# Feed-forward experts turned so that their rows lie on the partitions, with group weights multiplied in by GpSimd

## The chip, the cores and the metric

One NeuronCore of one Trainium2 chip runs the whole program. The metric is device microseconds of one execution, median of the runs; a profiled execution gives the trace. The engines are TensorE (PE, with its weight loads shown as PEld), VectorE (DVE), ScalarE (ACT), GpSimd (POOL) and SyncE (SP), which here issues all DMAs. All matrix products are done in float32r by splitting each operand into a high and a low part and adding three products (high x high, high x low, low x high).

## The reference

Input x is 4 batches of 1024 tokens of 256. First a multi-head latent attention block with 16 heads is added to x; it is not touched by the change but for its last body. Then comes the feed-forward part on the layer norm of the result, for each token n:

```
scores = softmax(x @ gate_w.T)                     # 64 experts
w_e    = the 8 largest of scores, 0 elsewhere
flat   = w_e[:, inv_map]                           # 8 groups of 8
scalar = flat.sum(-1)                              # one weight per group
soft   = softmax(where(flat == 0, -1e9, flat), -1)
xg     = x[:, None, :] + einsum('ngi,ghi->ngh', soft, mask_up_w)
g, u   = xg @ gate_proj, xg @ up_proj              # 176 rows per group
d      = (silu(g) * u) @ down_proj
y      = sum over g of scalar[g] * d[g]
```

The 8 groups of 176 rows make 1408 = 11 x 128 rows. The kernel computes the gate and up product of xg as x times the weights plus soft times a small product of mask_up_w and the weights (the "mask weights", `mw`), made once at the start.

## The kernel before

`attention_prepare` and `attention` do the attention (lines 66 to 1562), `ffn` (line 1565 on) the rest. `attention` is written as bodies 0 to 32, one per pair of heads, in which each engine works through a list written out by hand (TENSOR, VECTOR, SCALAR, POOL, SYNC); the last body has lists of its own (TENSOR_LAST and so on, line 1004), which also hold the router steps R(0) to R(6) of the first half-batch, the splitting of the first quad of expert weights into high and low (QUAD), the mask product of that quad (MASK) and the statistics of the second half-batch (STATS). SP loads the second quad's weights at line 1258 and then stores the last batch's sums.

`ffn` works on 32 tiles of 128 tokens; four tiles are a half-batch H (8 of them), for which the router runs as a unit. Tokens lie on the partitions. For a tile i, PE does for each group g six matmuls of 352 columns (gate and up rows of the group side by side, `gate_up`, line 1652), the tile of x being the stationary operand. After four groups `soft` (line 1662) adds the mask part with four matmuls that use 32 rows each and run side by side. ScalarE takes the silu (line 1758), and VectorE multiplies gate, up and the token's group weight in one instruction (`gates`, line 1815; the group weight is one number per partition). For the down product the result has to be turned: `transposes` (line 1673) has PE turn 11 blocks of 128x128 into one bank, in steps of 4, 4 and 3; ScalarE copies the high part out (`high`, line 1764), VectorE subtracts to get the low part (`low`, line 1823), and PE does 11 x 3 matmuls of 256 columns (`down`, line 1689). VectorE adds the tile to x (`add_up`) and SP stores a half-batch at a time.

The order on PE is that of the loop at line 1706: gate/up of groups 0 to 7 of tile i, with the transposes and the down product of tile i-1 between them. The router's steps for the next half-batches are put between them by tables (PE_AT, ACT_AT, DVE_AT, line 1612) that give each step a tile and a place. The router's steps are `router_tensor`, `router_scalar` and `router_vector` (lines 672 to 808): PE parts 0 and 1 turn the normalised x, 2 makes the logits, 3 turns the selected weights, 4 gathers them by group, 5 and 6 turn the soft weights; VectorE's part 4 (lines 773 to 779) ends the softmax and finds the top 8, part 5 (lines 781 to 785) selects, part 6 makes the group weights, part 7 the soft weights. Layer norm is GpSimd's: `router_root` and four `router_norm` (lines 828 to 841); it does nothing else in this part apart from two subtractions at the start (line 1874).

## Time and profile before

| | us |
|---|---|
| median of 3 runs (1659.49 to 1663.20) | 1661.84 |
| the profiled execution's own time | 1660.86 |
| its span, first to last instruction | 1658.8 |
| PE busy in the span | 1565.8 |
| VectorE busy | 1181.2 |
| ScalarE busy | 814.4 |
| GpSimd busy | 806.3 |
| feed-forward part, from PE's first matmul at 1160.87 to the end | 497.9 |

Busy times are sums over one engine; they overlap with each other. A matmul's end is modelled, so durations of consecutive matmuls overlap: the distance between two starts is what a matmul costs. GpSimd's and ScalarE's times are as recorded.

### The profile page before, as it was taken

The numbers are of one execution on the slowest core, as the hardware profiler recorded it, in microseconds if no ns is written. First come the engines' busy times: TensorE is split into PE (matmuls) and PEld (weight loads), VectorE is DVE, ScalarE is ACT, GpSimd is POOL, SyncE is SP. The second block draws the span as 40 slices with busy tenths as digits, with TensorE's granted clock in tenths as the row PEclk, the third lists the DMA queues.
The fourth block names the chain that finished last, engine by engine and source line by source line (L and its number), as shares of the span: only waits on it lengthen the run. The fifth ranks groups of instructions, "written<-read, shape, count | busy, mean of one in ns | idle before, by whom it ended". The sixth has DMA issues, their size and how long they took to land. (4 is left out here: it accounts for less than half of the span.)

```text
span 1658.8 us, 69237 instructions
## 1 busy us (share of the span) xinstructions
PE 1565.8 (94%) x30224; PEld 1343.1 (81%) x30224; DVE 1181.2 (71%) x2780; ACT 814.4 (49%) x1902; POOL 806.3 (49%) x673
## 2 busy tenths in 40 slices
PE   5689999999999999999999999997999999999998
PEld 4568878877778777877877878875899999999998
DVE  6778878887788778878877888886645446445443
ACT  6555555555556555555555555543433333333332
POOL 4376767676667666676767676762010010011000
PEclk9889999999999999999999999998999999999999
DMA  9523221112231112222112311112100000000000
GB/s 299 130 71 79 55 54 45 52 41 73 72 77 53 48 51 77 64 64 73 55 45 63 93 42 42 45 39 77 59 27 1 26 27 1 26 27 1 13 14 13
DMA packets 83981, 91.87 MB, mean 55 GB/s; under 512 B 33696, under 2 KB 58272, under 8 KB 83680
## 3 DMA queue, kind: packets, MB, share of 16 engines
q1 hardware_dynamic: 83680, 87.44, 18.5%
q8 instruction: 240, 3.93, 1.0%
q14 instruction: 61, 0.50, 0.1%
HBM read 55.67 MB, written 14.94 MB: 43 GB/s over the span
## 5 line engine op out<-in xcount | busy, mean ns | idle before, releaser
L1395 ACT ACTIVATE probs<-aps,nmax 128x896 f32<-128x896 f32 (+7 forms) x512 | 378.1, 740 | 410.3 <-DVE nmax L1443 398.4
L1443 DVE CUSTOM_DVE_ANT_0 aps<-aps,mask_row 128x896 f32<-128x896 f32 (+7 forms) x512 | 380.7, 759 | 122.9 <-PE aps L46 119.4
L46 PE MATMUL aps<-kTh,qh 128*128 128x512 f32 (+3 forms) x768 | 291.2, 379 | 13.7 <-DVE ql L1131 7.2
L1122 POOL TENSOR_TENSOR rot<-rot,sinT 64x512 f32<-64x512 f32 x126 | 160.4, 1273 | 292.7 <-DMA rot<-rot 292.7
L46 PE MATMUL aps<-pT_second,vrep 32*64 32x128 f32 (+1 forms) x15616 | 263.5, 260 | 26.2 <-issue 23.3
L46 PEld LDWEIGHTS aps<-pT_second,vrep 32*64 32x64 f32 x15616 | 224.8, 131 | 66.1 <-issue 53.7
L1453 DVE STREAM_TRANSPOSE pT_second<-probs 128x896 f32<-128x896 f32 (+3 forms) x256 | 264.0, 1032 | 4.7 <-ACT probs L1395 4.5
L46 PE MATMUL aps<-kTl,qh 128*128 128x512 f32 (+3 forms) x768 | 259.2, 345 | 1.6 <-issue 1.6
L46 PE MATMUL aps<-kTh,ql 128*128 128x512 f32 (+3 forms) x768 | 223.2, 345 | 0.0
L46 PEld LDWEIGHTS aps<-kTh,qh 128*128 128x128 f32 x768 | 145.5, 189 | 75.0 <-issue 38.9
L1826 DVE TENSOR_TENSOR aTl<-fps,aTh 128x512 fp32r<-128x512 f32 (+1 forms) x96 | 61.9, 646 | 167.3 <-ACT aTh L1769 167.3
L46 PE MATMUL fps<-wth,qh 128*128 128x352 f32 x512 | 176.1, 344 | 3.7 <-PEq L848 3.7
L1769 ACT CAST aTh<-fps 128x512 fp32r<-128x512 f32 (+1 forms) x96 | 52.8, 551 | 235.7 <-PE fps L1685 235.6
L1453 DVE STREAM_TRANSPOSE pT_first<-probs 128x256 f32<-128x256 f32 (+3 forms) x256 | 124.1, 495 | 59.1 <-ACT probs L1395 58.9
L46 PE MATMUL fps<-wtl,qh 128*128 128x352 f32 x512 | 166.1, 324 | 0.0
L46 PE MATMUL fps<-wth,ql 128*128 128x352 f32 x512 | 165.8, 324 | 0.0
L831 POOL TENSOR_SCALAR f_vareps<-f_aggr 128x4 f32<-128x4 f32 x8 | 1.9, 233 | 336.1 <-DVE f_aggr L759 336.1
L1125 POOL TENSOR_TENSOR rot<-rot 64x512 f32<-64x512 f32 x126 | 160.4, 1273 | 9.9
L1131 POOL TENSOR_TENSOR ql<-rot,qh 128x512 fp32r<-128x512 f32 x126 | 159.7, 1285 | 7.4 <-ACT qh L1384 7.4
L1123 POOL TENSOR_TENSOR rot<-rot,cosT 64x512 f32<-64x512 f32 x126 | 161.3, 1280 | 0.0
L46 PEld LDWEIGHTS aps<-kTl,qh 128*128 128x128 f32 x768 | 146.6, 191 | 12.4 <-issue 0.2
L46 PEld LDWEIGHTS aps<-kTh,ql 128*128 128x128 f32 x768 | 137.2, 191 | 8.9
(195 smaller groups left out, 3032.9 us busy)
## 6 DMA issues: line engine op xcount, KB each, us to landing
rot<-rot SPq DMA_DIRECT2D x256, 64.0 KB, 2.5
linv_b<-inverses_scratch SPq DMA_DIRECT2D x128, 128.0 KB
wqs<-wq_scratch SPq DMA_DIRECT2D x30, 256.0 KB, 3.6
raw_numbers<-in_x SPq DMA_DIRECT2D x8, 512.0 KB, 6.4
vrep<-values_scratch SPq DMA_DIRECT2D x16, 256.0 KB, 4.6
inverses_scratch<-linv_t SPq DMA_DIRECT2D x256, 1.0 KB
acc<-in_x SPq DMA_DIRECT2D x16, 256.0 KB, 3.2
x_scratch<-acc SPq DMA_DIRECT2D x16, 256.0 KB, 3.1
```

Source lines behind the costliest of these rows:

```text
L46: return nc.tensor.matmul(out, lhsT, rhs, start=start, stop=stop, skip_group_check=True)
L831: pool.tensor_scalar(t.vareps[:], t.aggr[:, :, 1], EPS, None, ALU.add).then_inc(t.ve, 1)
L1122: eng.tensor_tensor(rot2[:, k, :], rot2[:, k, :], t.sinT[:, cols], ALU.mult).then_inc(q_turned, 1)
L1123: eng.tensor_tensor(rot1[0:64, k, :], rot1[0:64, k, :], t.cosT[0:64, cols], ALU.mult).then_inc(q_turned, 1)
L1125: eng.tensor_tensor(rot1[0:64, k, :], rot1[0:64, k, :], rot2[:, k, :], ALU.add).then_inc(q_add, 1)
L1131: eng.tensor_tensor(ql[:, a, cols], rot1[:, rot_slot(x, r), :], qh[:, a, cols].bitcast(F32), ALU.subtract).then_inc(q_split, 1)
L1395: nc.scalar.activation(probs[:, SLOT[x, r], 0:w], sps[:, at:at + w], ACT.Exp, bias=nmax[:, c, a, j:j + 1], scale=-1.0, accum_out=lsum[:, c ...
L1443: nc.vector.tensor_tensor_reduce(out=s, in0=s, in1=mask[:, N - PW[c][j]:N], scale=-1.0, scalar=3.0e38, op0=ALU.add, op1=ALU.min, accum_out ...
L1453: nc.vector.transpose(pT[c][:, a, 0:w // S32, j * S32:(j + 1) * S32], probs[:, SLOT[EXP(c, a, j), r], 0:w].rearrange("p (b k) -> p b k", k ...
L1769: nc.scalar.copy(aTh[:, i % 2, m.start:m.stop, :].rearrange("p m n -> p (m n)"), turned_in(i, q)[:, 0:len(m) * P]).then_inc(aT_h, 1)
L1826: nc.vector.tensor_tensor(aTl[:, i % 2, m.start:m.stop, :].rearrange("p m n -> p (m n)"), turned_in(i, q)[:, 0:len(m) * P], aTh[:, i % 2, ...
```

## The change

In the feed-forward part tokens move to the free axis. The work is cut into 8 half-batches x 11 blocks of 128 expert rows = 88 blocks (n = 11 H + m). For a block PE multiplies the block's 128 gate rows (stationary) with 512 tokens, six matmuls of 512 columns, then the same for its up rows; `soft` adds the mask part with one full-height matmul of 512 columns for each (two for block 5, which has rows of groups in both halves of the soft weights). For that the mask weights are laid out with zeros in all rows but those of a block's groups (`mwz`, in the space of the attention's keys). 8 of the blocks lie in a single group; blocks 4, 5 and 10 are put together from three, four and three groups (MIXED). The down product needs no transposes: its stationary operand is the block's product, 128 tokens at a time, 4 x 3 matmuls of 256 columns, added up over 11 blocks in two banks. It follows two blocks behind (LAG).

The group weight is now different along the free axis, so it can't be one number per partition. VectorE multiplies up and silu (`gate`), GpSimd multiplies the result with a spread tile of weights (`weigh`), ScalarE rounds it to the high part, VectorE subtracts for the low part. The spread tiles come by DMA: VectorE's part 6 turns the group sums in squares of 32, SP writes them to DRAM in 4 DMAs and reads them back spread over the partitions, 18 DMAs per half-batch. The router's steps get a block in place of a tile (`router_parts`); the statistics of the half-batch after next come at block 8, its layer norm on GpSimd at blocks 9 and 10. The mask products are taken over column ranges (pure groups 256 columns, mixed blocks 2 x 48). The first quad's weights are loaded in three pieces, not four, and the down weights are loaded in attention's last body.

The diff, cut to its core:

```diff
+WORDS = [5 * KC * GB, 6 * KC * GB]
+FIRST_QUAD, SECOND_QUAD = (0, 2, 1), (1, 0, 2, 3)
+MIXED = {4: [(0, slice(0, 48), P), (1, slice(48, 96), P), (2, slice(96, P), P)],
+         5: [(2, slice(0, 16), 160), (3, slice(16, 64), P), (4, slice(64, 112), P), (5, slice(112, P), P)],
+         10: [(5, slice(0, 32), 144), (6, slice(32, 80), P), (7, slice(80, P), P)]}
+SOFT = [[(0, m)] for m in range(5)] + [[(0, 5), (1, 5)]] + [[(1, m)] for m in range(5)]
...
 def mask_products(nc, t, q, bank):
-        for gg in range(4):
-            last = mm(nc, bank[32 * gg:32 * gg + 32, 0:GU], t.mu4[:, k, g, :], columns(part, g, k).bitcast(F32),
+        for g, m, first, width, at in mask_windows(q):
+            last = mm(nc, to, t.mu4[:, k, g, :], both_columns(part, m, k, slice(first, first + width)).bitcast(F32),
...
+def mask_clear(nc, t, q):
+    nc.gpsimd.memset(t.kTh[:, q, :].bitcast(F32), 0.0).then_inc(t.mw_zero, 1)
+    nc.gpsimd.memset(t.kTl[:, q, 0:2 * GB].bitcast(F32), 0.0).then_inc(t.mw_zero, 1)
+def mask_spread(nc, t, q):
+            nc.gpsimd.tensor_copy(to, src).then_inc(t.mw_rdy, 1)
+            copied += 1
+            nc.gpsimd.wait_ge(t.mw_rdy, copied)
+def keep_mass(nc, t, H):
+    nc.sync.wait_ge(t.mass_turned, H + 1)
+    to = t.mass_dram[H % 2].rearrange("g (t a i) -> a (g t) i", a=4, i=32)
+    for a in range(4):
+        nc.sync.dma_start(to[a], t.massT[32 * a:32 * a + 32, :]).then_inc(t.mass_kept, 16)
...
+        if H > 0:
+            dve.wait_ge(t.mass_kept, 64 * H)
+        dve.transpose(t.massT[:], t.mass[:, H % 2]).then_inc(t.mass_turned, 1)
...
             load_experts(nc, t, ins, 1, slice(0, 4))
+            sp.wait_ge(t.first_low, len(PIECES[0]))
+            sp.dma_start(t.raw_d, ins["down"].rearrange("(m p) d -> p m d", p=P)).then_inc(t.down_loaded, 16)
+            keep_mass(nc, t, 0)
             all_added(LAST - 1)
...
+        PE_AT = {0: 0, 1: 1, 2: 2, 3: 4, 4: 5, 5: 8, 6: 9}
+        ACT_AT = {0: 0, 1: 1, 2: 3, 3: 4, 4: 6, 5: 8, 6: 9}
+        DVE_AT = {1: 0, 2: 1, 3: 2, 4: 3, 5: 3, 6: 5, 7: 6}
...
+            def spread_mass(H, m):
+                if H > 0:
+                    sp.wait_ge(weighted, (H - 1) * MC + m + 1)
+                for g, rows, _ in MEMBERS[m]:
+                    row = t.mass_dram[H % 2, g]
+                    sp.dma_start(mass_b[rows, m, :], row.partition_broadcast(rows.stop - rows.start))\
+                        .then_inc(mass_loaded[m], 16)
...
+            def products(n, u):
+                if n >= 2:
+                    pe.wait_ge((silu_done, act_done)[u], n - 1)
                 for k in range(KC):
+                    for j, (x, w) in enumerate(((t.xTh, t.wth), (t.xTh, t.wtl), (t.xTl, t.wth))):
+                        mm(nc, banks[:, 2 * (n % 2) + u, :], columns(w, m, k, u), x[:, k, tok(H)], k == 0 and j == 0, False)
+            def soft(n, u):
+                for q, e in entries:
+                    last = mm(nc, banks[:, 2 * (n % 2) + u, :], t.mwz[q][e][:, u * P:(u + 1) * P], t.sT[:, q, tok(H)],
+                              False, (q, e) == entries[-1])
+            def down(n):
+                pe.wait_ge(aT_l, n + 1)
+                for i in range(HT):
                     for j, (a, w) in enumerate(((aTh, dh), (aTh, dl), (aTl, dh))):
+                        last = mm(nc, y_of(i), a[:, n % SLOTS, i * P:(i + 1) * P], w[:, m, :], m == 0 and j == 0 and i % 2 == 0,
+                                  m == MC - 1 and j == 2)
...
+                elif n < TOTAL:
+                    for u in range(2):
+                        products(n, u)
+                        soft(n, u)
+                    parts(n)
+                if n >= LAG:
+                    down(n - LAG)
...
+            for n in range(TOTAL):
+                silu(n)
+                if n > 0:
+                    high(n - 1)
+                parts(n)
...
+            def gate(n):
+                dve.wait_ge(up_ps, n + 1)
+                dve.wait_ge(silu_done, n + 1)
+                if n >= SLOTS:
+                    dve.wait_ge(aT_h, n - SLOTS + 1)
+                nc.vector.tensor_tensor(act_sb[:, n % SLOTS, :], banks[:, 2 * (n % 2) + 1, :], sg[:, n % SLOTS, :],
+                                        ALU.mult).then_inc(act_done, 1)
+            def low(n):
+                dve.wait_ge(aT_h, n + 1)
+                nc.vector.tensor_tensor(aTl[:, n % SLOTS, :], act_sb[:, n % SLOTS, :],
+                                        aTh[:, n % SLOTS, :].bitcast(F32), ALU.subtract).then_inc(aT_l, 1)
...
+            def weigh(n):
+                pool.wait_ge(act_done, n + 1)
+                pool.wait_ge(mass_loaded[m], 16 * len(MEMBERS[m]) * (H + 1))
+                nc.gpsimd.tensor_tensor(act_sb[:, n % SLOTS, :], act_sb[:, n % SLOTS, :], mass_b[:, m, :], ALU.mult)\
+                    .then_inc(weighted, 1)
...
+            for n in range(TOTAL):
+                weigh(n)
+                if m in (9, 10) and H + 2 < HALVES:
+                    if m == 9:
+                        router_root(nc, t, H + 2)
+                        pool.wait_ge(t.xT_ps, 2 * H + 4)
+                    for i in range(2 * (m - 9), 2 * (m - 9) + 2):
+                        router_norm(nc, t, H + 2, i)
```

VectorE's loop runs gate(n), low(n-1), then the router parts of block n, and at block 1 the four sums of the half-batch before.

## Rows read from the trace of the kernel before

**Rows 1.** The page's part 1, busy time by engine.
```profile
PE 1565.8 (94%) x30224; PEld 1343.1 (81%) x30224; DVE 1181.2 (71%) x2780; ACT 814.4 (49%) x1902; POOL 806.3 (49%) x673
```
**Rows 2.** Windows: stretch, length, busy by engine, granted clock, DMA share, GB/s.
```profile
1242.43:1303.96 61.53, 60.92 (x444) 57.29 (x443) 31.51 (x93) 22.38 (x55) 6.81 (x6) 1.00 0.06 18
...
1640.00:1659.00 19.00, 14.01 (x106) 12.81 (x104) 6.07 (x15) 3.83 (x12) 0.00 (x0) 1.00 0.05 15
```
**Rows 3.** PE groups by form, 1242.43 to 1303.96: busy, mean ns, idle before.
```profile
L46 PE MATMUL fps<-dh,aTh 128*128 128x256 f32 x44 | 13.2, 300 | 0.6 <-DVE aTl L1826 0.6
```
**Rows 4.** Timeline of PE, 1249 to 1255: start, length, what.
```profile
1249.78 0.28 PE L46 MATMUL fps<-dh,aTh 128*128 128x256 f32 x1
...
1250.84 0.32 PE L46 MATMUL fps<-wth,qh 128*128 128x352 f32 x1
...
1253.74 0.60 PE L1685 MATMUL fps<-ident,act_sb 128*128 128x128 f32 x4
1254.27 0.44 PE L46 MATMUL fps<-mw,xq 32*128 32x352 f32 x4
1254.63 0.43 PE L46 MATMUL fps<-wth,qh 128*128 128x352 f32 x1
1254.90 0.32 PE L46 MATMUL fps<-wtl,qh 128*128 128x352 f32 x1
```
**Rows 5.** The chain that ended last, 1227 to 1228: start, length, what.
```profile
1227.23 0.44 PE fps L1685 x4
```
**Rows 6.** Timeline of PE in attention, 603 to 604.
```profile
602.97 1.09 PE L46 MATMUL aps<-xq,wqs 128*128 128x512 f32 x4
603.89 0.40 PE L46 MATMUL aps<-kTh,qh 128*128 128x512 f32 x1
```
**Rows 7.** Groups by form: VectorE and ScalarE 1183 to 1645, GpSimd whole span.
```profile
L1826 DVE TENSOR_TENSOR aTl<-fps,aTh 128x512 fp32r<-128x512 f32 x61 | 42.1, 691 | 112.7 <-ACT aTh L1769 112.7
...
L1769 ACT CAST aTh<-fps 128x512 fp32r<-128x512 f32 x61 | 35.8, 587 | 172.9 <-PE fps L1685 172.9
...
L1541 POOL TENSOR_TENSOR ol<-o,oh 128x512 fp32r<-128x512 f32 x64 | 82.5, 1288 | 32.4 <-ACT oh L1405 32.4
```
**Rows 8.** Timelines of VectorE and GpSimd at 1163, and VectorE at 1284.
```profile
1162.84 2.94 DVE L807 TENSOR_TENSOR rot<-mask_row,soft_h 128x256 f32<-128x256 f32 x2
...
1163.00 2.50 POOL L1874 TENSOR_TENSOR wtl<-raw_numbers,wth 128x1024 fp32r<-128x1024 f32 x1 [11.53 <-DVE rot L804]
...
1284.27 0.76 DVE L807 TENSOR_TENSOR rot<-mask_row,soft_h 128x256 f32<-128x256 f32 x2
```
**Rows 9.** Timeline of VectorE: first and last of router parts 4 and 5.
```profile
1190.02 0.42 DVE L774 TENSOR_REDUCE r<-mask_row 128x4 f32<-128x256 f32 x1
...
1191.81 0.06 DVE L63 MEMSET f_spot_v<- 1x1 f32 x1
...
1196.33 0.08 DVE L782 MATCH_VALUE_LOAD mask_row<-top,mask_row 128x8 f32 x1
...
1197.23 0.42 DVE L785 TENSOR_TENSOR mask_row<-mask_row 128x256 f32<-128x256 f32 x1
```
**Rows 10.** Timeline of GpSimd at one layer norm: root's first step, the four norms.
```profile
1133.95 0.23 POOL L831 TENSOR_SCALAR f_vareps<-f_aggr 128x4 f32<-128x4 f32 x1 [5.71 <-DVE f_aggr L759]
...
1135.41 4.96 POOL L840 TENSOR_SCALAR cosT<-x,f_aggr,f_rstd 128x256 f32<-128x256 f32 x4
```
**Rows 11.** Timeline of PE: mask products of groups 4 to 7, and what follows.
```profile
1168.58 0.80 PE L46 MATMUL fps<-wth,mu 128*32 128x352 f32 x8
...
1171.09 0.43 PE L46 MATMUL fps<-wth,qh 128*128 128x352 f32 x1
```
**Rows 12.** Timeline at the end: PE's last matmul, VectorE's last add.
```profile
1655.84 0.28 PE L46 MATMUL fps<-dh,aTl 128*128 128x256 f32 x1
1656.16 0.42 DVE L1834 TENSOR_TENSOR x<-fps,x 128x256 f32<-128x256 f32 x1 [2.37 <-PE fps L46]
```

468 lines of the change are left out of this document (223 added, 245 removed).

## The prediction

> **What bounds the kernel now.** I read the page first, then the stretch of the feed-forward part (1161 us to the end) by windows, by groups and by time. On the page TensorE (PE) is busy for 1565.8 us of a span of 1658.8 us [rows 1]. In the feed-forward part one half-batch (512 tokens, four tiles) takes the 61.53 us from 1242.43 to 1303.96, of which PE is busy 60.92 us at a granted clock of 1.00 (2.4 GHz); VectorE has 31.5 us, ScalarE 22.4 us and GpSimd 6.8 us of work in it [rows 2]. Only 0.6 us of idle stands in front of the down matmuls [rows 3]. So this part costs what PE issues, and the change is to be priced by PE's pace, then by whether the other engines still keep ahead of it. Ends of matmuls are modelled, so I take distances between starts: nine 256-column down matmuls fill 1249.78 to 1250.84, 0.118 us each, and eighteen 352-column ones 1250.84 to 1253.74, 0.161 us each [rows 4]. Four transposes take 0.44 us [rows 5].
>
> **PE, per half-batch.** Before: 4 tiles x 8 groups x 6 = 192 gate/up matmuls of 352 columns, 192 x 0.161 = 30.9 us. After: 11 blocks x 2 x 6 = 132 of 512 columns. 512-column matmuls run in attention: four from 602.97 to 603.89, so 0.230 each [rows 6]; I take 0.232, and 132 x 0.232 = 30.6 us. The columns are the same (67,584) and so, almost, is the time: minus 0.3 us.
> The 44 transposes of the products go away, since the products now come out with the expert rows on the partitions: minus 11 x 0.44 = 4.8 us.
> The eight soft-mask groups were four 32-row matmuls each, which ran side by side: 0.36 us from 1254.27 to 1254.63. The matmul behind each took 0.27 us instead of 0.16, and the four transposes ahead of it 0.53 us instead of 0.44 [rows 4, 5]. So 8 x (0.36 + 0.11 + 0.09) = 4.5 us go. In their place come 24 full-height matmuls of 512 columns (twelve windows, gate and up): plus 24 x 0.232 = 5.6 us. Here the change pays: zero rows are multiplied too.
> The down product stays at 132 matmuls of 256 columns, the router's steps keep their instructions. The 0.6 us wait before down matmuls should go, as there are now two blocks between a product and its use.
> Sum: -0.3 - 4.8 - 4.5 + 5.6 - 0.6 = **-4.6 us per half-batch**, 8 x 4.6 = 36.8 us.
>
> **The new chain per block.** PE needs 14 x 0.232 + 12 x 0.118 = 4.66 us for a block. Call T(n) the time at which block n's up product is complete. Its products are needed by the down matmuls that PE reaches at T(n+2), 9.3 us later. Nearest rows: VectorE's 128x512 with one operand in PSUM 0.69, ScalarE's cast 0.59, GpSimd's 128x512 multiply-like operation 1.29 [rows 7]. VectorE's product is done at T(n) + 0.7, GpSimd's at + 2.0, ScalarE's high part after its silu of block n+1 at about + 4.2, VectorE's low part after the gate of n+1 at + 6.0. That leaves 3 us, so a plain block does not stall.
>
> **Where VectorE and GpSimd meet.** The new low part (act_sb minus aTh) reads two operands in SBUF, and begins just when GpSimd's multiply of the next block, with two SBUF operands as well, is released. The row to read is VectorE's pair of 128x256 subtractions at 1162.84, both operands in SBUF: 2.94 us for two that elsewhere take 0.76 us together; it ends at 1165.78, just behind GpSimd's 2.50 us operation, 1163.00 to 1165.50 [rows 8]. So I let the two exclude each other, first come first served: GpSimd's multiply ends at T(n) + 2.65, still inside the slack. The Trainium skill, "SBUF — State Buffer", section "Who interferes with whom", states it so: a VectorE instruction with two SBUF inputs and a GpSimd one that reads SBUF take turns, the second blocked for the whole of the first. The trace agrees (2.94 us against 0.76); by the rule as by the row the sum holds the two stalls that follow, and with ports of their own it would be that of the first rival. Two places remain where this reaches PE:
> (a) Block 3, router top-k. VectorE does gate, low part, part 4 and part 5, and PE's part 3 waits for the result at T(4) = T(3) + 4.66. Part 4 takes 1.85 us and part 5 1.3 us [rows 9]; gate and low part take 1.4 us, and the first two-operand step of part 4 (due at T(3) + 2.05) waits for GpSimd until about T(3) + 2.65, a loss of 0.6 us. Result at T(3) + 5.2 or a little later: PE waits 0.6 us, 7 times = **+4.2 us** (0 to 1.5 each).
> (b) Blocks 9 and 10, layer norm of the half-batch after next on GpSimd. Root takes 1.5 us and four norms 5.0 [rows 10], now mixed with two multiplies: multiply of 9 ends at T(9) + 2.65, root at + 4.15, two norms at + 6.65, multiply of 10 (behind VectorE's low part, which has waited for the second norm) at + 8.65, two norms at + 11.15. PE's transposes of it stand at T(9) + 2 x 4.66 + 0.44 = + 9.8. PE waits 1.35 us, for six half-batches = **+8.1 us** (0 to 2.5 each).
>
> **Data movement.** The group weights now go by DMA: VectorE turns the 128x32 masses in 32x32 squares, 4 issues put them to DRAM, then 18 spreading reads per half-batch (2.9 MB) fetch them, issued on SP from block 5 on and due from the next half-batch's block 0. That is five blocks, 23 us, to spare. On SP they stand behind the store and load of x, whose next user is block 8's statistics, and each read waits for the multiply that last used its tile, in the order of the blocks. I cost them nothing. If one is late, GpSimd's multiply stands first, and behind it ScalarE, VectorE and PE. In the last attention body SP waits for the turned masses ahead of the last stores of x; VectorE makes them before the adds that these stores wait for, so nothing again. The down weights are loaded in that body, behind the expert loads, and not in the feed-forward part: they were hidden and stay so.
>
> **Start and end.** The mask products for groups 4 to 7 cover 256 + 96 + 96 = 448 columns in place of 352, in the same side-by-side form; they took 2.5 us, 1168.58 to 1171.09 [rows 11], so +0.7 us. The first blocks share their engines with the expert splitting, 18 small mask copies on GpSimd, each waited for, and a clear. The trace has no such copy. Below, they cost nothing; above, 18 at the 1.29 us of rows 7 for the widest are 23 us, of which a block's slack hides at least 15, so 8 us. I take +0.3 us, near the low end because the narrow ones have a quarter of the partitions, PE has 18 to 24 matmuls to do first, and the first tile's present waits go. Together +1.0 us. At the end, PE's last matmul starts at 1655.84, one add of 0.42 us follows at 1656.16, and the span ends at 1658.8 [rows 12]. Now four adds stand there (+1.3 us). PE is idle for some 2.1 us in the last tile (5.0 us of the last 19, less the 2.9 after its end [rows 2]) and will be for 1.2 us, before the last block's down product: -0.9. Together +0.4 us.
>
> **Sum.** 1658.8 - 36.8 + 4.2 + 8.1 + 1.0 + 0.4 = 1635.7 us of span. The profiled execution took 1660.86 us, 2.1 us more than its span, and lies 1 us below the median of the runs (1661.84). So 1637.8 to 1638.8; I say **1638 us**. About 0.2% (3.3 us) is what a measurement of this kernel can tell from no change.
>
> **Rivals.**
> 1. No stall of (a) and (b): GpSimd and VectorE fall into another order, or PE's own small losses cover them. 1638 - 12.3 = about 1625 us. For: the times above are within 1 us of cover. Against: (b) counts busy time of GpSimd, not only waits. 0.22.
> 2. The 512-column matmuls are slower here than in attention, or block-wise switches between product, soft and down cost something. At 0.245 us each, 156 x 0.013 = 2.0 us per half-batch, 16 us, so 1654 us. For: the first matmul of several groups in attention is longer (first after a switch 0.27 here [rows 4]). Against: the 0.230 of rows 6 is of a run of four. 0.12.
> 3. Slower than before: the chain of one block misses its two-block slack, so that PE waits in every block. It has to exceed 9.3 us by 0.3 us to cost 88 x 0.3 = 26 us and lose all. With GpSimd's multiply and VectorE's work queuing behind each other in each block (say gate 0.7, multiply 1.3, low 0.7, multiply again delayed) I reach 7.4 us; it takes a multiply of over 3.2 us in place of 1.29 [rows 7] to decide. At 3.6 us, 88 x 0.5 = 44 us, 1680 us. 0.09.
> 4. The change does not do what it says, in that the weights do not ride along for free: the spread tiles arrive late and PE starves at the begin of a half-batch. It takes a delay of 23 us of cover plus 3 us; then 7 x 3 = 21 us, 1659 us, the same as before. 0.05.
> The forecast itself (one or both stalls, 1630 to 1648) has 0.52.
>
> **Numbers.** Faster: forecast, rivals 1 and 2 = 0.86, less 0.02 for sizes off, 0.84; same 0.05; slower 0.11. The range takes in rivals 1 and 2 and leaves out the rest: 1620 to 1656.
>
> **What the changed profile would show.** Feed-forward half-batch near 58.6 us instead of 61.5; wth matmuls of 512 columns at starts 0.232 us apart; no transposes of act_sb; GpSimd 40 to 50% busy in this part, its multiply recorded as 1.3 to 1.9 us; idle before the PE transposes of wsel (0.6 us) and of the normalised x (1.3 us). Wrong would be: idle before each down matmul naming aTl (rival 3), 512-column starts 0.245 apart (rival 2), waits of GpSimd on the spread DMA (rival 4).

## The result and the profile after

The changed kernel takes 1635.89 us, median of four runs (1634.12 to 1638.19), beside 1660.66 us (1659.18 to 1663.20) for the kernel before in the same set: a ratio of 0.985, with an interval of 0.983 to 0.987. So the change makes the kernel 1.5% faster, clear of the noise and small. The prediction said 1638 us, range 1620 to 1656, so the time came out 2 us below it. Below it will be seen that this closeness is in part luck: two terms were off in opposite directions. Of the executions of the kernel before that stand beside the experiments, one (in the set of e9 to e11) took 3703.11 us and counts as slow; the ratios leave it out.

The profiled execution took 1634.89 us, span 1632.8 us. The head of its page, and the three groups of it that belong to the change (the group's columns: line, engine, operation, out<-in, count, busy and mean ns, idle before and its releaser; then the two DMA groups, with KB and us from issue to landing):

```profile
span 1632.8 us, 68005 instructions
PE 1534.4 (94%) x29424; PEld 1279.1 (78%) x29424; DVE 1157.3 (71%) x2609; ACT 802.2 (49%) x1725; POOL 956.6 (59%) x783
...
L1940 POOL TENSOR_TENSOR act_sb<-act_sb,mass_b 128x512 f32<-128x512 f32 x88 | 143.4, 1630 | 265.5 <-DVE act_sb L1885 265.4
...
mass_b<-mass_scratch SPq DMA_DIRECT2D x64, 256.0 KB, 3.8
mass_b<-mass_scratch SPq DMA_DIRECT2D x48, 96.0 KB, 3.8
```

Against [rows 1] TensorE has 31.4 us less to do and GpSimd 150 us more, nearly all of it the 88 multiplies. Their mean of 1630 ns, against the 1.29 us of the operation that I priced them by [rows 7], is the first thing to explain. Of the 265.5 us that GpSimd idles ahead of them, 265.4 end with VectorE's gate (line 1885), none with a DMA: the spread weights are never late.

The windows of the changed kernel, one for two whole half-batches each, one for the last 19 us (columns: length, busy us and instructions of PE, PE's weight loads, VectorE, ScalarE and GpSimd, then PE's granted clock, DMA share and GB/s):

```profile
1240.04:1297.70 57.66, 57.24 (x332) 49.29 (x331) 28.37 (x72) 20.85 (x33) 24.03 (x17) 1.00 0.23 70
1297.70:1355.40 57.70, 57.28 (x332) 49.32 (x331) 28.39 (x72) 20.85 (x33) 24.03 (x17) 1.00 0.23 69
1614.00:1633.00 19.00, 13.74 (x85) 11.90 (x83) 5.58 (x11) 2.83 (x5) 5.00 (x3) 0.98 0.08 28
```

A half-batch takes 57.7 us in place of 61.53 [rows 2], a gain of 3.9 us. The two half-batches differ by 0.04 us: inside the feed-forward part the profile repeats itself far better than whole executions do, and so most of the readings below are made on it. GpSimd is busy for 24.0 of 57.7 us, 42% (forecast 40 to 50%). What PE still waits for in that part, over all eight half-batches (columns: us in total, times, longest):

```profile
PE fps L47 <- PEq L920: 3.3, 1, 3.3
PE fps L751 <- POOL cosT L912: 2.4, 6, 1.0
PE fps L47 <- DVE aTl L1892: 0.8, 1, 0.8
PE fps L47 <- ACT sg L1837: 0.7, 1, 0.7
```

The 3.3 us is the way from attention into the feed-forward code, 3.7 before. The wait for aTl, which stood 9 times for 6.0 us in all before (0.6 us of it in each half-batch, [rows 3]), is there once, at the very end. New is the wait for the normalised x (cosT, the stall (b) of the prediction): six times, but 2.4 us in all and not 8.1. A wait for mask_row, stall (a), is too short for this list; the group of its transposes shows 0.1 us of idle per half-batch. The listed idle times are less than PE loses: a 512-column matmul is followed by the next start after 0.23 us, but by the transposes of mask_row after 0.53 (0.13 of it listed as idle) and by those of cosT after 0.68 in five of the six cases (0.28 listed). The stalls below are read from these distances. PE's groups in the first window:

```profile
L47 PE MATMUL fps<-qh,wtl 128*128 128x512 f32 x44 | 17.4, 396 | 0.0
L47 PE MATMUL fps<-qh,wth 128*128 128x512 f32 x44 | 17.4, 396 | 0.0
L47 PE MATMUL fps<-ql,wth 128*128 128x512 f32 x44 | 17.3, 394 | 0.0
...
L751 PE MATMUL fps<-ident,cosT 128*128 128x128 f32 x8 | 1.3, 280 | 0.3 <-POOL cosT L912 0.3
...
L767 PE MATMUL fps<-ident,mask_row 128*128 128x128 f32 x2 | 0.4, 301 | 0.1
```

44 + 44 + 44 = 132 gate/up matmuls of 512 columns, as forecast, and no transposes of act_sb. (The 396 ns are modelled ends; the pace is read from starts, below.)

**Where the time came from.** I divide each profiled execution at the first feed-forward matmul. Before: 1160.87, then 497.91 us to the end of the span. After: 1164.11, then 468.67 us. So the feed-forward part gives 29.2 us, where the prediction had 36.8 - 4.2 - 8.1 - 1.0 - 0.4 = 23.1. And the part ahead of it takes 3.2 us more, where the prediction had 0. These two differences are what the experiments are about.

### The profile page after: what moved, and what is told of

Read it like the earlier page. It is cut to its first block and busy times, and to the rows that moved or that the text cites. A ratio compares the mean times of both kernels' runs of the same rounds, so it can differ in the third digit from the quotient of the medians.

```text
span 1632.8 us, 68005 instructions
## 1 busy us (share of the span) xinstructions
PE 1534.4 (94%) x29424; PEld 1279.1 (78%) x29424; DVE 1157.3 (71%) x2609; ACT 802.2 (49%) x1725; POOL 956.6 (59%) x783
## 5 line engine op out<-in xcount | busy, mean ns | idle before, releaser
L1940 POOL TENSOR_TENSOR act_sb<-act_sb,mass_b 128x512 f32<-128x512 f32 x88 | 143.4, 1630 | 265.5 <-DVE act_sb L1885 265.4
L1885 DVE TENSOR_TENSOR act_sb<-fps,sg 128x512 f32<-128x512 f32 x88 | 60.8, 691 | 225.1 <-PE fps L47 222.2
L1837 ACT ACTIVATE sg<-fps 128x512 f32<-128x512 f32 x88 | 52.6, 597 | 247.7 <-PE fps L47 247.7
L47 PE MATMUL fps<-qh,wth 128*128 128x512 f32 x352 | 140.3, 399 | 4.0 <-PEq L920 3.3
L47 PE MATMUL fps<-qh,wtl 128*128 128x512 f32 x352 | 140.1, 398 | 0.0
L47 PE MATMUL fps<-ql,wth 128*128 128x512 f32 x352 | 139.3, 396 | 0.0
```

The costliest lines, as they stand in the source:

```text
L47: return nc.tensor.matmul(out, lhsT, rhs, start=start, stop=stop, skip_group_check=True)
L1837: nc.scalar.activation(sg[:, n % SLOTS, :], banks[:, 2 * (n % 2), :], ACT.Silu).then_inc(silu_done, 1)
L1885: nc.vector.tensor_tensor(act_sb[:, n % SLOTS, :], banks[:, 2 * (n % 2) + 1, :], sg[:, n % SLOTS, :], ALU.mult).then_inc(act_done, 1)
L1940: nc.gpsimd.tensor_tensor(act_sb[:, n % SLOTS, :], act_sb[:, n % SLOTS, :], mass_b[:, m, :], ALU.mult)\
```

## The experiments

All kernels carry one edit to the changed kernel (e10 and e11: to the kernel before). "FF" is the length of the feed-forward part in the profiled execution, "half-batch" the distance between the same router transposes in two consecutive half-batches, "last body" the stretch from the last attention body's mask_row transposes to the first feed-forward matmul.

| kernel | time, us (runs) | last body | FF | half-batch |
|---|---|---|---|---|
| before | 1660.66 (4) | 12.36 | 497.91 | 61.53 |
| after | 1635.89 (4) | 14.19 | 468.67 | 57.68 |
| e1 multiply with one input | 1638.73 (4) | 15.40 | 469.93 | 57.97 |
| e2 multiply on VectorE | 1633.82 (4) | 13.90 | 466.74 | 57.45 |
| e3 low part ahead of the gate | 1636.70 (4) | 14.91 | 467.06 | 57.48 |
| e4 norm a block earlier | 1637.43 (4) | 14.71 | 464.79 | 57.17 |
| e5 down weights loaded late | 1630.85 (1) | 11.46 | 469.05 | 57.68 |
| e6 group weights spread once | 1634.50 (1) | 14.93 | 468.75 | 57.71 |
| e7 no soft mask from half-batch 1 | 1599.59 (1) | 13.95 | 440.26 | 54.03 |
| e8 e3 + e4 + two sums | 1627.59 (4) | 14.36 | 462.58 | 56.90 |
| e9 e8 + e5 | 1627.85 (6) | 12.94 | 463.90 | 56.90 |
| e10 before, no soft mask from tile 4 | 1651.00 (1) | 11.44 | 482.51 | 59.38 |
| e11 before, fewer transposes | 1632.09 (1) | 10.41 | 475.27 | 58.39 |

Five of these kernels do not compute the full result: e1 leaves out the group weights, e6 takes those of the first half-batch for all, e7 and e10 leave out the mask part, e11 uses products that were not turned. They are there to be timed. The medians of the kernel before beside them were 1666.67 us (e1 to e4), 1659.73 (e5 to e8) and 1660.80 (e9 to e11). A whole execution moves by several us from one to the next: the last attention body's first router transposes stand anywhere from 1122.5 to 1136.6 us in these profiles, in code that no experiment changes. TensorE's granted clock moves as well. In each of these profiles it drops to the lower of its two levels (1.2 and not 2.4 GHz) for some stretches of the last attention body: over the "last body" of the table the mean clock is 0.76 before, 0.72 after, 0.79 in e5 and 0.63 in e9. Behind the first router transposes of the feed-forward part the mean is 1.00 in all of them. So differences of 1 to 4 us are read from the feed-forward part, and only their sum (e8) from the times.

### e1: does GpSimd's multiply hold VectorE up through its second input?

```
-   nc.gpsimd.tensor_tensor(act_sb[...], act_sb[...], mass_b[:, m, :], ALU.mult)
+   nc.gpsimd.tensor_scalar(act_sb[...], act_sb[...], 1.0, None, ALU.mult)
```

> Changed kernel, but GpSimd's multiply in the feed-forward part has one tensor input in place of two (act_sb times 1.0, so the group weights are left out of the result). Theory: only a GpSimd instruction with two tensor inputs shuts out VectorE's two-input instructions in SBUF (one-input norms at 1282.4 to 1283.6 did not delay VectorE's low part at 1283.0). Then GpSimd's multiply is no longer stretched from 1.29 to 1.67 us by the low part beside it, router part 4's division (0.83 us in the changed kernel) is back at 0.42, PE's 0.13 us wait before part 3 goes, and the time falls by 1 to 3 us from 1636. Rival (the page's rule: any GpSimd instruction that reads SBUF): the division stays at 0.6 to 0.8 us, the instruction is stretched by 0.4 us as now, and the time stays.

Measured: 1638.73 us (1633.33 to 1645.95), ratio 0.9836 [0.9793, 0.9879]; FF 469.93, 1.3 us longer and not shorter. First the meeting in block 3 as the changed kernel has it, VectorE (start, duration, line, operation, idle before):

```profile
1246.72 0.69 DVE L1885 TENSOR_TENSOR act_sb<-fps,sg 128x512 f32<-128x512 f32 x1 [2.98 <-PE fps L47]
1247.33 0.68 DVE L1892 TENSOR_TENSOR aTl<-act_sb,aTh 128x512 fp32r<-128x512 f32 x1
...
1248.62 0.83 DVE L844 TENSOR_TENSOR mask_row<-mask_row,r 128x256 f32<-128x256 f32 x1
...
1251.04 0.42 DVE L853 TENSOR_TENSOR mask_row<-mask_row 128x256 f32<-128x256 f32 x1
```

and GpSimd at the same time, in the changed kernel:

```profile
1247.49 1.67 POOL L1940 TENSOR_TENSOR act_sb<-act_sb,mass_b 128x512 f32<-128x512 f32 x1 [4.82 <-DVE act_sb L1885]
```

The multiply is released while the low part (1247.33 to 1248.01) runs, and takes 1.67 us: 1.29, and 0.38 behind VectorE. It is under way until 1249.16, and the division of part 4 (L844, two operands in SBUF), started in its shadow at 1248.62, takes 0.83 in place of 0.42. In e1, on VectorE:

```profile
1257.15 0.68 DVE L1892 TENSOR_TENSOR aTl<-act_sb,aTh 128x512 fp32r<-128x512 f32 x1
...
1258.44 0.42 DVE L844 TENSOR_TENSOR mask_row<-mask_row,r 128x256 f32<-128x256 f32 x1
```

and on GpSimd:

```profile
1257.31 1.86 POOL L1940 TENSOR_SCALAR act_sb<-act_sb 128x512 f32<-128x512 f32 x1 [4.62 <-DVE act_sb L1885]
```

VectorE's division runs from 1258.44 to 1258.86, wholly inside a GpSimd instruction that ends at 1259.17, and is back at 0.42 us. So this GpSimd instruction with one SBUF tensor operand does not hold up VectorE's division; the one with two does. (The two differ in the operation too, TENSOR_SCALAR against TENSOR_TENSOR, so the operand count is the likely reason and not an isolated one.) Nor is one operand always free: in the same profile five low parts that start 0.28 us into a norm take 0.80 or 0.81 us in place of 0.68, which is still far from waiting out the 0.94 us that the norm had left. The other direction is not so: the one-operand instruction is itself stretched when it starts behind VectorE's low part. It takes 1.49 us where nothing of VectorE stands before it and 1.86 here. The half of the theory that expected shorter times fell on a plain fact: GpSimd takes longer over this one-operand form than over the two-operand one (1.49 against 1.29 us), so stall (b) grew (cosT, 6 times, 6.0 us in all) while the wait for mask_row went away (its transposes stand 0.24 us behind the last soft matmul, with no idle).

### e2: is GpSimd needed for the multiply at all?

```
    gate(n): ... act_sb = up * sg                              (VectorE)
+            nc.vector.tensor_tensor(act_sb[...], act_sb[...], mass_b[:, m, :], ALU.mult)
-   weigh(n) on GpSimd
```

> The multiply by the spread group weights done by VectorE, behind its product, in place of GpSimd; nothing else changed. Theory (PE bound, two blocks of slack): no plain block stalls; the wait for the layer norm (0.29 us, six times) goes as GpSimd is free; router part 4 has no lock any more (minus 0.41 us) but VectorE does 0.69 us more ahead of it, so PE waits 0.3 to 0.6 us before part 3, seven times. Sum within 2 us of 1636. Rival (GpSimd's help is needed, VectorE would bind): PE waits before down products in every block, 10 us or more slower.

Measured: 1633.82 us (1632.24 to 1635.29), ratio 0.9804 [0.9779, 0.9829]; FF 466.74, 1.9 us shorter than in the changed kernel. PE's waits, feed-forward part of e2:

```profile
PE fps L767 <- DVE mask_row L853: 2.9, 7, 0.4
```

The multiply takes 0.69 us on VectorE, ahead of the router parts, so that PE's wait before the transposes of mask_row grows to 0.4 us, seven times; in exchange cosT is never waited for. VectorE is busy for half of a half-batch (28.4 of 57.7 us in the changed kernel), so 11 x 0.69 us more is no load. Having the multiply on GpSimd is no gain here: on VectorE it takes slack in block 3, on GpSimd in blocks 9 and 10, and the second was the scarcer.

### e3: the low part ahead of the gate

```
 for n in range(TOTAL):
+    if n > 0: low(n - 1)
     gate(n)
-    if n > 0: low(n - 1)
```

> VectorE does the low part of block n-1 ahead of the product of block n, not behind it (its input is ready 0.5 us before the product's). Theory (low part and multiply exclude each other): the multiply is recorded as 1.29 us everywhere in place of 1.67, router part 4 starts 0.6 us earlier against an end of the multiply only 0.3 us earlier, PE's wait before part 3 goes (0.9 us over seven) and the last block's chain is 0.3 us shorter: 1 to 3 us faster than 1636. Rival (the 1.67 is GpSimd's own time on this shape): the multiply stays at 1.67.

Measured: 1636.70 us (1631.44 to 1639.59), ratio 0.9818 [0.9788, 0.9848]; FF 467.06 (-1.6). The gate releases GpSimd's multiply; with the low part in front of the gate the low part and the multiply no longer meet. GpSimd's group in the half-batch from 1240 to 1297 us of e3:

```profile
L1940 POOL TENSOR_TENSOR act_sb<-act_sb,mass_b 128x512 f32<-128x512 f32 x11 | 14.2, 1291 | 37.3 <-DVE act_sb L1885 37.3
```

1291 ns against the 1630 of the changed kernel: this answers the question of the first fence. The wait for mask_row is gone, though the division behind the multiply still takes 0.55 us in most half-batches, and not 0.42. The wait for cosT has grown a little, though (PE's waits, the whole feed-forward part of e3):

```profile
PE fps L751 <- POOL cosT L912: 3.1, 6, 1.4
```

GpSimd's multiply ends 0.4 us sooner, but the low part now comes to stand where a norm is released, and stretches it: the first pair of norms takes 2.75 us in this half-batch of e3 and 2.43 in the changed kernel. The meeting is moved, not removed.

### e4: the layer norm a block earlier

```
-   if m == 8 and H + 2 < HALVES:   statistics of x (VectorE)
+   if m == 7 and H + 2 < HALVES:
...
-   if m in (9, 10) and H + 2 < HALVES:   root, then two norms behind each multiply (GpSimd)
+   if m in (8, 9) and H + 2 < HALVES:
```

> Statistics of the half-batch after next at block 7 in place of 8, its layer norm on GpSimd at blocks 8 and 9 in place of 9 and 10. Theory (b): PE's waits for the normalised x go, 2.4 us of idle plus its restart: 2 to 3 us faster than 1636, feed-forward half-batch 57.4 us in place of 57.7. Rival: the wait moves to another step (statistics before the top of router part 7, or PE's part 5), time the same.

Measured: 1637.43 us (1631.96 to 1638.04), ratio 0.9816 [0.9783, 0.9848]; FF 464.79, 3.9 us less. The waits for cosT are gone, and a half-batch of e4 reads:

```profile
1240.00:1297.18 57.18, 57.05 (x331) 49.39 (x330) 28.27 (x72) 20.83 (x33) 24.03 (x17) 1.00 0.24 70
```

PE busy for 57.05 of 57.18 us; 0.13 us is left, stall (a). So stall (b) costs 3.9 us over the kernel (1.2 us between the first two router transposes, 48.53 against 47.31, and 0.5 in each of the five half-batches after it). That is more than the 2.4 us that the list of waits gives. The starts show most of the rest: in the changed kernel the transposes of cosT stand 1.40 us behind the matmul ahead of them the first time and 0.68 the other five, in e4 0.23 each time, which makes 3.4 us. The prediction had 8.1. Why it is half, GpSimd shows in the changed kernel, in blocks 9 and 10:

```profile
1278.05 1.67 POOL L1940 TENSOR_TENSOR act_sb<-act_sb,mass_b 128x512 f32<-128x512 f32 x1 [3.46 <-DVE act_sb L1885]
1279.69 0.23 POOL L903 TENSOR_SCALAR f_vareps<-f_aggr 128x4 f32<-128x4 f32 x1
1280.00 1.04 POOL L905 TENSOR_TENSOR f_rstd<-f_vareps,minus_half 128x4 f32<-128x4 f32 x1
1281.21 2.43 POOL L912 TENSOR_SCALAR cosT<-x,f_aggr,f_rstd 128x256 f32<-128x256 f32 x2 [0.18 <-POOL f_rstd L905]
1283.61 1.29 POOL L1940 TENSOR_TENSOR act_sb<-act_sb,mass_b 128x512 f32<-128x512 f32 x1
1284.88 2.42 POOL L912 TENSOR_SCALAR cosT<-x,f_aggr,f_rstd 128x256 f32<-128x256 f32 x2
```

and VectorE beside it, in the changed kernel, blocks 9 and 10:

```profile
1277.27 0.69 DVE L1885 TENSOR_TENSOR act_sb<-fps,sg 128x512 f32<-128x512 f32 x1 [2.11 <-PE fps L47]
1277.88 0.68 DVE L1892 TENSOR_TENSOR aTl<-act_sb,aTh 128x512 fp32r<-128x512 f32 x1
1282.41 0.69 DVE L1885 TENSOR_TENSOR act_sb<-fps,sg 128x512 f32<-128x512 f32 x1 [3.85 <-PE fps L47]
1283.02 0.68 DVE L1892 TENSOR_TENSOR aTl<-act_sb,aTh 128x512 fp32r<-128x512 f32 x1
```

T(9) is 1277.08, where PE's last matmul of block 9's up product gives way to the next. Up to the second norm all goes as forecast: multiply of 9 done at T(9) + 2.64 (said 2.65), root at + 4.13 (4.15), two norms at + 6.56 (6.65). The prediction let VectorE's low part of block 10 wait for the second norm and GpSimd's next multiply wait for the low part. But the low part starts at 1283.02, in the middle of that norm, and takes its plain 0.68 us; the multiply starts at 1283.61, as the norm ends, and takes its plain 1.29 us. It ends at T(9) + 7.8, not + 8.65, and the last norm at T(9) + 10.2, not + 11.15. The norm has one tensor operand in SBUF and is a TENSOR_SCALAR, as the multiply of e1 is. PE, changed kernel, at the point where it comes to the normalised x:

```profile
1286.68 0.40 PE L47 MATMUL fps<-xq,kTh 128*128 128x512 f32 x1
1287.36 0.66 PE L751 MATMUL fps<-ident,cosT 128*128 128x128 f32 x4 [0.29 <-POOL cosT L912]
```

A 512-column matmul further on is 1286.68 + 0.23 = 1286.91, T(9) + 9.8, as the prediction had it. The start at 1287.36 is 0.45 us behind it: that is the stall of one half-batch, predicted 1.35.

### e5: the down weights loaded where they were

```
     load_experts(nc, t, ins, 1, slice(0, 4))
-    sp.wait_ge(t.first_low, len(PIECES[0]))
-    sp.dma_start(t.raw_d, ins["down"]...)
...
     spread_mass(0, m)            (SyncE, feed-forward part)
+    sp.dma_start(t.raw_d, ins["down"]...)
     load(2)
```

> One part of the change undone: the down weights are loaded at the start of the feed-forward part again, not in attention's last body. Theory A: the 1.44 MB load in the last body holds up PE's instruction fetch, which shows as a PE gap that waits for nothing ('issue', 2.2 to 3.7 us) inside the eight matmuls by onehot, in all runs of the changed kernel and not in the one before; without the load the gap is gone and from the last transposes of mask_row in attention to PE's first feed-forward matmul it takes some 12 us in place of 14.2 (11.9 to 12.4 before), while the feed-forward part itself is longer by 0 to 3 us, as the first down product waits. Theory B: the gap comes from the code's length and place alone; it stays.

Measured: 1630.85 us, one run. The last body takes 11.46 us in place of 14.19, FF 469.05 (+0.4). Of the 2.7 us, 2.27 are in one place; the rest is that PE is busy for 7.68 us of the stretch in place of 8.15, at a granted clock of 0.79 in place of 0.72. PE in the changed kernel ("issue" is a gap in which it waited for nothing that the profile shows):

```profile
1151.07 1.33 PE L47 MATMUL aps<-onehot,wselT 128*128 128x64 f32 x5 [0.46 <-ACT wselT L797]
1154.66 0.69 PE L47 MATMUL aps<-onehot,wselT 128*128 128x64 f32 x3 [2.27 <-issue]
```

and in e5:

```profile
1149.34 1.97 PE L47 MATMUL aps<-onehot,wselT 128*128 128x64 f32 x8 [0.46 <-ACT wselT L797]
```

Eight matmuls of one loop, with one wait ahead of all of them, are torn apart by 2.27 us. The same gap, between the fifth and the sixth of them, stands in each of the eight profiles with the early load (2.2 to 3.8 us: after 2.27, e1 2.68, e2 2.23, e3 3.75, e4 3.55, e6 3.68, e7 2.29, e8 3.11). Of the five without it, four (before, e5, e9, e10) have no gap there and e11 one of 0.52 us. Gaps named "issue" are not new as such: all thirteen profiles have one or two among the pT_second matmuls a few us earlier, the longest of each profile 2.0 to 4.9 us, before the change (2.77 and 2.04 us) as after it (3.84 and 0.67). Summed over the last attention body these gaps come to 3.8 to 4.8 us in the five profiles without the early load and to 6.8 to 7.9 us in the eight with it. In the changed kernel the load of the down weights is issued 4.8 us ahead of these matmuls:

```profile
1146.29 0.38 SPq L1330 DMA_DIRECT2D raw_down<-in_down  x1
```

In the eight profiles the gap ends 7.8 to 8.4 us behind this issue. That the load makes the gap is shown by its going and coming; the edit of e5 leaves PE's code as it is. How the load does it is not shown: no row here says what PE stands still for.

### e6: are the spread reads hidden?

```
-   dve.wait_ge(t.mass_kept, 64 * H)        +   dve.wait_ge(t.mass_kept, 64)
-   keep_mass(nc, t, H + 1), and the 11 spread_mass(H + 1, m) of each half-batch
-   pool.wait_ge(mass_loaded[m], 16 * len(MEMBERS[m]) * (H + 1))
+   pool.wait_ge(mass_loaded[m], 16 * len(MEMBERS[m]))
```

> The group weights are written to DRAM and spread once, for the first half-batch, and used for all (so half-batches 1 to 7 are weighted wrongly); the 2.9 MB per half-batch of spreading reads are gone. Theory: these transfers were hidden and cost nothing; half-batch 57.7 us as now, within 0.1. Rival: DMA writes beside PE slow it a little (256-column down matmuls start 0.120 us apart in the changed kernel against 0.118 before): 0.118 again, 0.3 us less per half-batch.

Measured: 1634.50 us, one run; FF 468.75 against 468.67, a half-batch 57.71 against 57.68. Taking some 20 MB of DMA away (7 x 2.9 MB) gives nothing, on any engine. Rival 4 has no ground, and the transfers are worth nothing, as costed.

### e7: the new soft mask taken out

```
 def products(n, u): (the last product closes the bank for H > 0)
 def soft(n, u):
+    if H > 0: return
```

> The soft-mask matmuls are left out for half-batches 1 to 7 (mask part missing from the result). Theory (PE bound, each 512-column matmul costs its pace of 0.234 us): 24 x 0.234 = 5.6 us less per half-batch, 57.7 becomes 52.1. Rival: the other engines, or the shorter block of 4.2 us, bind by then: 53 us or more, with waits of PE named aTl.

Measured: 1599.59 us, one run; a half-batch 54.03 us, 3.65 less, and not 5.6. The rival's "53 us or more" came true, but the waits do not name aTl. One half-batch, and PE's waits over the feed-forward part, in e7:

```profile
1233.34:1287.37 54.03, 51.68 (x309) 44.83 (x307) 28.22 (x73) 20.98 (x33) 24.14 (x18) 1.00 0.24 74
```

```profile
PE fps L751 <- POOL cosT L912: 10.3, 6, 1.8
PE fps L767 <- DVE mask_row L853: 3.6, 6, 0.6
```

PE's busy time falls from 57.24 to 51.68, by 5.56 us, which is 24 x 0.232: the term was sized to the hundredth. But a block is now 0.46 us shorter, GpSimd's and VectorE's work is not, and both stalls grow. The transposes of cosT stand 2.15 us behind the matmul ahead of them in place of 0.68, those of mask_row 0.98 in place of 0.53; these 1.9 us are what is given back. It is the clearest picture here of what the prediction's "cover" means. The two stalls are not fixed prices but differences between two chains, and they grow with every us that PE saves.

### e8: the kernel without the stalls

The edits of e3 and e4 together, and the last half-batch's four sums of 256 columns made as two of 512 (stored in two pieces):

```
-   for i in range(HT):          nc.vector.tensor_tensor(tile, y_of(i), tile, ALU.add)
+   for i in range(HT // 2):     nc.vector.tensor_tensor(tile, banks[:, 4 + i, :], tile, ALU.add)
```

> Three edits that the traces point to together: VectorE's low part ahead of the product, layer norm on GpSimd one block earlier, and the four sums of a half-batch as two of 512 columns (with the last store in two pieces, not three). Theory: no PE wait for mask_row or cosT is left, half-batch 56.9 us, feed-forward part 468.7 - 3.9 (layer norm) - 2.2 (order) - 0.3 (end) = 462.3 us; the time is 6 us below the changed kernel's. Rival: the low part in front delays products and so the chain; 464 us or more.

Measured: 1627.59 us (1623.94 to 1629.88), ratio 0.9801 [0.9766, 0.9837]; FF 462.58, 6.1 us less than in the changed kernel. One half-batch of e8:

```profile
1240.00:1296.90 56.90, 56.90 (x333) 49.40 (x332) 28.14 (x71) 20.83 (x33) 20.58 (x17) 1.00 0.25 71
```

PE is busy for all of it, and the length is the 61.5 - 4.6 = 56.9 us that the prediction's sum of PE's work comes to. Against e4 (57.17) the half-batch gives 0.27 us; seven times that, 1.9 us, is what stall (a) costs, predicted 4.2. (The two sums in place of four are in it as well, but the starts agree: the transposes of mask_row move from 0.53 to 0.25 us behind the matmul ahead of them.) All four runs lie below all four of the changed kernel, with the kernel before within 1 us in both sets (1659.73 and 1660.66); the two ratios' intervals touch at their ends.

### e9: e8 with the down weights loaded late

> The three edits of the best version so far and the down weights loaded in the feed-forward part again. Theory: attention's last body is 2 to 3 us shorter (no PE gap inside the onehot matmuls), the feed-forward part 462.6 + 0.4 = 463.0 us; 2 us better than that version, ratio to the kernel before near 0.979. Rival: the load moves the first down products' wait into view, nothing gained.

Measured: 1627.85 us (1626.84 to 1629.20, six runs), ratio 0.9794 [0.9767, 0.9820]: no gain over e8 that can be measured. The gap of 3.1 us among the onehot matmuls is gone, but the last body takes 12.94 us in place of 14.36 and FF is 463.90 in place of 462.58. The windows of the last body and of the stretch behind it, up to the first router transposes, say why, in e8:

```profile
1150.79:1165.15 14.36, 7.48 (x89) 5.47 (x87) 4.68 (x11) 3.35 (x7) 2.62 (x3) 0.76 0.34 113
1165.15:1203.71 38.56, 37.84 (x277) 31.25 (x278) 25.32 (x49) 18.63 (x28) 22.02 (x28) 0.96 0.38 103
```

and in e9:

```profile
1149.38:1162.32 12.94, 9.26 (x88) 6.45 (x87) 4.71 (x10) 3.26 (x7) 2.62 (x3) 0.63 0.13 42
1162.32:1202.17 39.85, 39.00 (x277) 31.91 (x278) 25.10 (x49) 18.64 (x28) 22.01 (x28) 0.93 0.46 136
```

In e9's profile PE was granted a lower clock in both stretches (0.63 against 0.76, 0.93 against 0.96), and the same matmuls took it 9.26 us in place of 7.48 in the first. In the second e9 is 1.3 us longer; e5, which makes the same move at an unchanged 0.96, is 0.4 us longer there, so some 0.9 us of the 1.3 go with the clock and not with the load. Whether the clock falls so in the other five runs no trace tells. In e5 the exchange was 2.7 against 0.4 us, with one run. So an early down load costs between nothing and 2.3 us; which, these runs leave open.

### e10 and e11: two removed terms, taken out of the kernel before

e10, the soft mask of the kernel before left out from its fifth tile on:

```
     for gg in range(4):          (soft groups, 32 rows each)
+    if i >= HT: return           (ahead of the loop; the last product closes the bank)
```

> The kernel before without its soft-mask matmuls from the second half-batch on (mask part missing from the result). Prediction's term: 8 x (0.36 + 0.11 + 0.09) = 4.5 us per half-batch, 61.53 becomes 57.0. Rival: the switch losses were not theirs, 8 x 0.36 = 2.9 us, 58.6; or other engines bind and idle of PE named aTl grows.

Measured: 1651.00 us, one run; a half-batch 59.38 us, 2.15 less than before, where the prediction priced this work at 4.5 us. PE's waits in that one half-batch of e10:

```profile
PE fps L46 <- DVE aTl L1831: 2.5, 4, 1.2
```

Before it was 0.6 us in one [rows 3]. So 1.9 us were cover for the chain from PSUM to aTl. PE's own share is 2.15 + 1.9 = 4.05 us: 8 x 0.36 = 2.9 for the matmuls, and 1.15 in place of the 1.6 that I gave to the slower neighbours. The losses at the change between 32-row and full matmuls are real, and were over-sized by 0.45 us.

e11, the transposes of act_sb cut from 4, 4 and 3 per tile to one for each of the three:

```
-   for m in blocks(q):
+   for m in blocks(q) if i < 2 or i == TILES - 1 else blocks(q)[0:1]:
```

> The kernel before with one transpose in place of 4, 4 and 3 in each step of tiles 2 to 30 (so most of the products used are stale). Prediction's term: 0.11 us a transpose, 32 fewer per half-batch: 3.5 us, 61.53 becomes 58.0. Rival: they lay in cover of the wait for VectorE's products, and PE waits for aTl or at the transposes instead: over 59.5.

Measured: 1632.09 us, one run; a half-batch 58.39 us. The window of one, in e11:

```profile
1235.30:1293.68 58.38, 57.45 (x412) 53.71 (x411) 31.43 (x93) 22.38 (x55) 6.81 (x6) 1.00 0.06 19
```

3.14 us less for 32 fewer transposes, and 0.93 us of idle where 0.6 was: 3.47 us of PE's own, 0.108 each. The prediction's 0.11 (0.44 for four, [rows 5]) is what they cost.

## Why the prediction was right, and where not

**PE's work per half-batch: the sum right, its terms less so.** Forecast -4.6 us to 56.9, measured 56.90 in e8, where nothing waits. Of the pieces that the prediction priced, three hold: gate/up 30.8 us for 132 matmuls (0.233 each; said 30.6), new soft 5.56 for 24 (e7; said 5.6), transposes 0.108 each (e11; said 0.11). The old soft term was too high: 4.05 (e10; said 4.5). To see the whole, add up the distances from each start to the next over one half-batch, before (1260.60 to 1322.13) and in e8 (1250.70 to 1307.59). The prediction's old soft term is split here: 2.9 us for its own matmuls, 0.9 for the gate/up matmuls behind them, 0.7 for the transposes ahead of them.

| | before | e8 | measured | said |
|---|---|---|---|---|
| gate/up, without waits | 32.4 | 30.8 | -1.6 | -1.2 |
| transposes | 4.6 | 0 | -4.6 | -5.5 |
| soft | 2.9 | 5.6 | +2.7 | +2.7 |
| down | 16.8 | 16.3 | -0.4 | 0 |
| router | 4.3 | 4.1 | -0.2 | 0 |
| wait for aTl | 0.6 | 0 | -0.6 | -0.6 |
| sum | 61.5 | 56.9 | -4.6 | -4.6 |

The transposes with their neighbours were taken 0.9 us too high, and what gate/up, down and router save together 1.0 too low; the sum holds because these cancel, and that is luck. The second comes from where the pace was read: the 0.161 and 0.118 us of [rows 4] hold inside a run of equal matmuls; but before the change the first gate/up matmul behind transposes takes 0.245 us, the first down matmul behind them 0.202 and the step from a down matmul to a soft group 0.208, so the averages are higher. In e8 a gate/up matmul behind down or soft ones takes 0.234 or 0.235 us, as inside a run: the new order has fewer changes that cost.

Rival 2, slower 512-column matmuls, is out. Starts of the changed kernel from the timeline of PE in block 3, then what follows:

```profile
1248.66 0.40 PE L47 MATMUL fps<-qh,wth 128*128 128x512 f32 x1
...
1250.99 0.40 PE L47 MATMUL fps<-xq,kTl 128*128 128x512 f32 x1
1251.52 0.44 PE L767 MATMUL fps<-ident,mask_row 128*128 128x128 f32 x2
```

From 1248.66 to 1250.99 are ten matmuls, 0.233 each, a soft one among them; at the rival's 0.245 it would be 2.45 us.

**Stall (a), predicted 4.2 us, measured about 1.9.** In the fence above the transposes stand 0.53 us behind the last soft matmul, where 0.23 would be without a wait: 0.3 us and not 0.6. The mechanism was the right one. Block 3's up product is complete at T(3) = 1246.52; the multiply ends at 1249.16, T(3) + 2.64, as forecast, and the division begins at + 2.10 (said 2.05). Its loss was mis-sized, 0.41 us and not 0.6, and the result is there at T(3) + 4.94 in place of + 5.2.

**Stall (b), predicted 8.1 us, measured 3.9 (e4).** The step that failed is "multiply of 10 (behind VectorE's low part, which has waited for the second norm)". The norm of GpSimd did not hold up VectorE's low part. I had taken the exclusion seen between two-operand instructions [rows 8] and put it on a one-operand one. By the Trainium skill, "SBUF — State Buffer", section "Who interferes with whom", any GpSimd instruction that reads SBUF is enough, and the second one is fully blocked. Where GpSimd's instruction has two operands the runs agree in kind (the division 0.83 against 0.42; the multiply 1.67 against 1.29 behind the low part). Where it has one and is under way first, they do not: VectorE's low part at 1283.02 takes 0.68 us, the division in e1 0.42 us, and the worst case beside a norm (e1) 0.81. The measurements decide: by that rule (b) would be the predicted 1.35 us, and it is 0.45 us, as above.

**Rivals.** Rival 1 (no stalls, 1625 us) did not come of itself, but e8 shows its number to be about right: 1627.6 us. What is missing is not located; taking the early down load away as well (e9, 1627.85 us) did not bring it. Rival 3, that a block's chain misses its slack, is out: aTl is waited for once, at the end, with nothing behind it to cover it, and not at all in the half-batches of e7, whose blocks are 0.46 us shorter. Rival 4 is out by e6.

**The start: +1.0 us predicted.** PE waits once for ScalarE's sg, 0.7 us, as it did before for another tile. The mask copies on GpSimd take 0.4 to 0.5 us each, nearer the low end as I said; the mask products take 3.2 us (2.5 + 0.7). The first half-batch was not taken apart further, so the +1.0 as a whole is not measured.

**The end: +0.4 us predicted.** In the changed kernel PE's last wait and VectorE's four adds:

```profile
1626.88 0.39 PE L47 MATMUL fps<-dh,aTh 128*128 128x256 f32 x1 [0.83 <-DVE aTl L1892]
```

```profile
1628.61 1.42 DVE L1899 TENSOR_TENSOR x<-fps,x 128x256 f32<-128x256 f32 x4 [1.79 <-PE fps L47]
```

From PE's last matmul to the end are 4.5 us in place of 2.9, which is 0.3 more than the 1.3 that I gave for three more adds; the wait ahead of the last block is 0.8 us and not the 1.2 forecast. These cancel.

**The attention part: predicted 0, measured +3.2 us.** Here I costed "down weights are loaded in that body" at nothing, because I looked only at who waits for the data. 2.27 us are the gap that e5 takes away; 1.8 us is by how much the last body is longer in all. The remaining 1.4 us arose earlier: the first router transposes of the last body stand at 1127.72 before and 1129.44 after. By the diff, the only work up to there in which attention differs is one load of expert weights that the changed kernel leaves out, and this point moves by far more than that from profile to profile, so these 1.4 us are not shown to be the change's.

**The sum.** Feed-forward part: 36.8 - 1.9 - 3.9 = 31.0 us; 29.2 were measured, which leaves 1.8 for start and end together, where the prediction had 1.4. The stalls were taken 6.5 us too dear and attention 3.2 us too cheap, of which 1.8 are shown to be in the last body; so that 1638 is only 2 us from 1635.9 is in part luck.

## What to carry to other kernels

A stall that comes from two chains with a small margin (here 9.8 us of PE's work against 10.2 of GpSimd's) is not a fixed price. Work both ends out from starts in the trace, and expect each us saved on the main engine to bring part of itself back as waiting, as in e7, until the side chain is moved too (e8: two edits of order and two wider sums in place of four, 6 us in the feed-forward part with the same work).

A pace read inside a run of equal matmuls misses what the changes between kinds cost. Add up the distances between starts over a whole iteration and see that they close with its length.

Before giving work to an idle engine, ask what slack it spends: the multiply cost PE less on VectorE, busy for half of the time without it, than on GpSimd (e2), and the order of two instructions on VectorE decided where the two engines met (e3).

When whole executions scatter by several us, look for a stretch of the trace that repeats itself to 0.04 us, and judge small edits there; and compare the granted clock of two stretches before their lengths (e9).

## What was not expected of the hardware

Who holds up whom between VectorE and GpSimd depended here on the form of GpSimd's instruction and on who came first. A two-operand GpSimd instruction under way: VectorE's two-operand instruction waits (the division 0.83 us in place of 0.42; the one low part of the changed kernel that starts inside such a multiply, at 1180.22, takes 1.12 in place of 0.68). A one-operand norm or multiply under way: it mostly does not (0.42 and 0.68 us, e1 and the norm), and by 0.13 us at most (0.81, e1). GpSimd's small one-operand casts are an exception not followed up: one low part beside two of them (at 1191.86 in the changed kernel) took 0.85 us. VectorE's two-operand instruction under way: either GpSimd form is stretched (1.29 to 1.67 us, 1.49 to 1.86 us).

A one-operand 128x512 multiply takes GpSimd longer than a two-operand one, 1.49 against 1.29 us.

A load of the down weights issued 3.5 to 4.9 us ahead of a row of eight small matmuls tears it apart by 2.2 to 3.8 us, in eight profiles out of eight, with no semaphore in between.
